# First maxima over 128 rows, and the layer-norm roots of later batches as Newton steps on VectorE

## What is computed

```python
def _layernorm(x, axis=-1, eps=1e-05):
    m = jnp.mean(x, axis=axis, keepdims=True)
    v = jnp.var(x, axis=axis, keepdims=True)
    return (x - m) / jnp.sqrt(v + eps)
...
        q = apply_rotary_emb(q, cos, sin)
        k = apply_rotary_emb(k, cos, sin)
...
        scores = jnp.einsum('bhid,bhjd->bhij', q, k, preferred_element_type=jnp.float32) * scale
        scores = jnp.where(causal, scores, -jnp.inf)
        probs = jax.nn.softmax(scores, axis=-1).astype(x.dtype)
        out = jnp.einsum('bhij,bhjd->bhid', probs, v, preferred_element_type=jnp.float32).astype(x.dtype)
...
    x = x + _layernorm(_L0_attn_ref(_layernorm(x, axis=-1), ...), axis=-1)
```

## Time and profile before

| | us |
|---|---|
| median of 3 runs | 1308.08 (1306.36 to 1308.83) |
| the profiled execution | 1310.2 |
| its span | 1308.5 |
| first scores of slot 0 | 87.35 |
| first scores of slots 1, 2, 3, 4 | 143.27, 203.29, 262.07, 320.32 |
| busy: PE, DVE, ACT, POOL | 1163.0, 996.1, 932.6, 950.4 |

### The profile page before, as it was taken

How to read it: one execution, slowest core, us unless ns; L and a number is a source line. 1 busy time by engine, 2 the same in 40 slices (tenths; PEclk the granted TensorE clock), 3 DMA queues, 4 the chain that set the end, 5 groups by cost and what they waited for, 6 DMA issues and landing times. The chain is left out here.

```text
span 1308.5 us, 34679 instructions
## 1 busy us (share of the span) xinstructions
PE 1163.0 (89%) x13520; PEld 784.9 (60%) x13520; DVE 996.1 (76%) x2157; ACT 932.6 (71%) x2057; POOL 950.4 (73%) x988
## 2 busy tenths in 40 slices
PE   4689999999999999999999999999997398898983
PEld 1236676666666676766666676766776254564651
DVE  7859787877878787877879787877843748786857
ACT  3168878778786878778787878779897565454543
POOL 3529988898888888898888889888675425554524
PEclk8559999999999999999999999999999599998997
DMA  6541515253351515253342515253200400000002
GB/s 197 125 119 44 131 37 128 67 130 85 80 130 34 130 35 130 66 130 76 89 118 46 131 35 130 66 130 81 52 3 3 135 2 1 2 1 0 0 1 65
DMA packets 50635, 96.91 MB, mean 74 GB/s; under 512 B 6704, under 2 KB 23344, under 8 KB 48432
## 3 DMA queue, kind: packets, MB, share of 16 engines
q1 hardware_dynamic: 50480, 94.81, 29.6%
HBM read 58.47 MB, written 34.60 MB: 71 GB/s over the span
## 5 line engine op out<-in xcount | busy, mean ns | idle before, releaser
L651 POOL TENSOR_TENSOR Plo<-P,Phi 128x512 f16<-128x512 f32 (+3 forms) x640 | 538.6, 868 | 141.3 <-ACT P L389 140.7
L386 ACT ACTIVATE Phi<-psS 128x512 f16<-128x512 f32 (+3 forms) x768 | 383.4, 499 | 162.5 <-PE psS L254 114.7
L389 ACT ACTIVATE P<-psS 128x512 f32<-128x512 f32 (+3 forms) x640 | 305.5, 478 | 0.0
L272 PE MATMUL psO<-V,Plo 128*128 128x65 f16 x2304 | 287.8, 194 | 0.0
L268 PE MATMUL psO<-V,Phi 128*128 128x65 f16 x2304 | 287.5, 192 | 0.0
L270 PE MATMUL psO<-V,Phi 128*128 128x64 f16 x2304 | 287.2, 192 | 0.0
L248 PE MATMUL psS<-Q,K 128*128 128x512 f16 (+3 forms) x768 | 251.4, 327 | 37.6 <-DVE Plo L509 32.0
L558 DVE TENSOR_REDUCE pmax<-psX 128x1 f32<-128x512 f32 x384 | 254.8, 684 | 25.8 <-PE psX L330 15.9
L251 PE MATMUL psS<-Q,K 65*128 65x512 f16 (+3 forms) x768 | 251.7, 328 | 0.0
L330 PE MATMUL psX<-K,Q 128*128 128x512 f16 (+5 forms) x768 | 232.1, 337 | 18.6 <-DVE pmax L558 7.0
L268 PEld LDWEIGHTS psO<-V,Phi 128*128 128x128 f16 x2304 | 218.7, 98 | 39.8 <-POOL Plo L651 4.1
(11 more groups left out here) (163 smaller groups left out, 2180.0 us busy)
## 6 DMA issues: line engine op xcount, KB each, us to landing
K<-k_way SPq DMA_DIRECT2D x48, 512.0 KB, 6.9
k_way<-HL SPq DMA_DIRECT2D x64, 256.0 KB, 3.9
q_way<-HL SPq DMA_DIRECT2D x60, 256.0 KB, 3.8
Q<-q_way SPq DMA_DIRECT2D x60, 256.0 KB, 7.1
Q<-q_way SPq DMA_DIRECT2D x15, 512.0 KB, 11.9
x<-in_x SPq DMA_DIRECT2D x4, 512.0 KB, 5.5
out<-x SPq DMA_DIRECT2D x8, 256.0 KB, 2.2
y<-in_x SPq DMA_DIRECT2D x3, 512.0 KB, 10.5
```

What stands on the lines that cost most here:

```text
L272: mm = nc.tensor.matmul(O, M.Plo[:, U % NP_, k * P:(k + 1) * P], V[:, HD:2 * HD + 1], start=False, stop=j == t, skip_group_check=True)
L386: nc.scalar.activation(M.Phi[:, U % NP_, 0:w], X, ACT.Exp, scale=SCALE)
L389: nc.scalar.activation(full, X, ACT.Exp, scale=SCALE).then_inc(S.exp_done, 1)
L651: nc.gpsimd.tensor_tensor(M.Plo[:, U % NP_, 0:w], M.P32[:, U % NP_, 0:w], M.Phi[:, U % NP_, 0:w], ALU.subtract).then_inc(S.lo_pool, 1)
```

## The change

- The maxima of heads 1, 2 and 3 before slot 0 contract all 128 rows; TensorE waits for the second copy of Q ahead of head 1. Head 0 keeps 64 rows.
- The bn_stats of the three later batches move from u = 4 to u = 45 of s = -1, behind the maxima.
- bn_aggr, root and shift of each of these batches become 16 small steps of DVE, one at the start of each step u = 4 to 19 of slots 0, 2 and 3. The inverse root is a guess made with integer arithmetic on the bits and four Newton steps of three instructions; each waits for the one before. ACT's Sqrt at s = -1 and DVE's reciprocal there are gone.
- `x_normal` moves from u = 26 to 33 of s = -1 (24 tiles) to u = 30 to 37 of slots 0, 2 and 3 (8 tiles each).
- The rotary sums of K of the second head group (two items) move from POOL to DVE.

```diff
-X_STATS, X_RECIPROCAL, X_NORMAL = 4, 9, 26
-
+X_STATS = 45
+X_ROOT = {1: (0, 4), 2: (2, 4), 3: (3, 4)}
+X_NORMAL = 30
+
+DVE_SUMS = 6
...
+def inverse_root(nc, M, then, tiles):
+
+
+    std, rstd, half = M.std[:, tiles], M.rstd[:, tiles], M.shift[:, tiles]
+    then(nc.vector.tensor_scalar(rstd.bitcast(I32), std.bitcast(I32), -0.5, ROOT_SEED, ALU.mult, ALU.add))
+    yield
+    for _ in range(NEWTON):
+        then(nc.vector.scalar_tensor_tensor(out=half, in0=rstd, scalar=-0.5, in1=rstd, op0=ALU.mult, op1=ALU.mult))
+        yield
+        then(nc.vector.tensor_tensor(half, half, std, ALU.mult))
+        yield
+        then(nc.vector.scalar_tensor_tensor(out=rstd, in0=half, scalar=1.5, in1=rstd, op0=ALU.add, op1=ALU.mult))
+        yield
...
                     h, k = a
+                    if (s, h, k) == (-1, 1, 0):
+                        pe.wait_ge(S.first_twin, 16)
...
-                    rows = HD if s < 0 else P
+                    rows = HD if s < 0 and h == 0 else P
...
             def x_normal(n):
+                act.wait_ge(S.x_root, n // TT)
...
-                if s == -1 and u == X_STATS:
-                    act.wait_ge(S.var_ready[0], 3)
-                    nc.scalar.activation(M.std[:, TT:NT], M.std[:, TT:NT], ACT.Sqrt).then_inc(S.std_ready[0], 1)
-                if s == -1 and X_NORMAL <= u < X_NORMAL + TT:
-                    if u == X_NORMAL:
-                        act.wait_ge(S.rstd_ready[0], 1)
-                    for k in range(B - 1):
-                        x_normal(TT + (B - 1) * (u - X_NORMAL) + k)
+                for batch in range(1, B):
+                    if s == X_ROOT[batch][0] and X_NORMAL <= u < X_NORMAL + TT:
+                        x_normal(batch * TT + u - X_NORMAL)
...
+            def x_root(batch):
+
+
+                tiles = slice(batch * TT, (batch + 1) * TT)
+                for t in range(batch * TT, (batch + 1) * TT):
+                    last = nc.vector.bn_aggr(M.mv[:, t, :], M.bn[:, t, :])
+                then(last)
+                yield
+                then(nc.vector.tensor_scalar(M.std[:, tiles], M.mv[:, tiles, 1], EPS, None, ALU.add))
+                yield
+                yield from inverse_root(nc, M, then, tiles)
+                nc.vector.scalar_tensor_tensor(out=M.shift[:, tiles], in0=M.mv[:, tiles, 0], scalar=-1.0,
+                                               in1=M.rstd[:, tiles], op0=ALU.mult, op1=ALU.mult).then_inc(S.x_root, 1)
...
-                        if s == -2:
+                        if r < DVE_SUMS:
                             taken(dve, item)
...
-                    variance(range(TT, NT))
-                    dve.wait_ge(S.consts, 3)
-                if s == -1 and u == X_RECIPROCAL:
-                    x_reciprocal()
+                    for t in range(TT, NT):
+                        last = nc.vector.bn_stats(M.bn[:, t, :], M.y[:, t, :])
+                    then(last)
+                for batch in range(1, B):
+                    if s == X_ROOT[batch][0] and u >= X_ROOT[batch][1]:
+                        next(roots[batch], None)
...
-                if s == -2:
+                if r < DVE_SUMS:
                     return
```

More of the change, by code:

```diff
@@ L29 @@
 BF16 = mybir.dt.bfloat16
+I32 = mybir.dt.int32
 ALU = mybir.AluOpType
@@ L45 @@
 EPS = 1e-5
+ROOT_SEED = float(0x5F3759DF)
+NEWTON = 4
 NEG = -1.0e30
@@ L575, in join_max @@
                     dve.wait_ge(S.aux_free[(number[last] - k) % NAUX], (number[last] - k) // NAUX + 1)
+                if s < 0:
+                    dve.wait_ge(S.consts, 3)
                 nc.vector.tensor_reduce(M.pmax[:, 1, :, 2:7:4], M.pmix[:, :, 0:2, 0:3], AX.X, ALU.max)
@@ L612, in out_scale @@
                                         ALU.mult).then_inc(S.out_scaled, 1)
+            roots = {batch: x_root(batch) for batch in range(1, B)}
             for half in range(2):
@@ L1476, in build @@
         S.norm_later = sem("norm_later")
+        S.x_root = sem("x_root")
         S.y_stats = sem("y_stats")
```

## The result

| | before | after |
|---|---|---|
| median, us (4 runs each) | 1307.83 (1306.36 to 1308.83) | 1320.49 (1319.35 to 1324.85) |
| the profiled execution | 1310.2 | 1319.53 |
| its span | 1308.5 | 1317.8 |

The ratio is 1.0103, interval 1.0088 to 1.0117: the changed kernel is slower by 12.7 us. Its lines have moved: first scores L248 → L269, maxima L330 → L353 with the mask at L334 → L357, the projections L304 → L325, exponentials L386 and L389 → L409 and L412, low parts L651 → L682, the later bn_stats L477 → L661, normals L438 → L462. The root is at L179 to L186, its shift at L529.

What follows compares the result with a forecast made beforehand. The prediction took TensorE to bound the kernel, at half clock in the start and with DVE, POOL and ACT close behind in the slots. Terms -7.0 + 16.8 + 4.8 = +14.6 on 1308.1 gave 1322.7 us, range 1309 to 1332.

Steps and rivals of the forecast that it cites:

- The start: Before slot 0: moved statistics and 128-row maxima together make slot 0 begin 7.0 us earlier, near 80.3; ends 4.2 and 8.7.
- Statistics: Before slot 0: without the 24 bn_stats, V's banks come free sooner and the second group of maxima starts 4.2 us earlier.
- 128 rows: Maxima of heads 1 to 3: full rows let TensorE's clock rise some 8 us into head 1, saving 2.8 us.
- products with the same columns cost the same at one clock: First maxima: going from 64 to 128 rows changes no product's cost at one clock; only the clock can change.
- The rival in which the clock stays low: Maxima before slot 0: no clock rise, the start gives only 4.2 us; +17.4 in all, 1325.5 us; chance 0.12.
- The roots: Steps 4 to 19 of slots 0, 2, 3: small DVE instructions wait for POOL's running one; together 16.8 us later.
- 0.64 x (18.14/16)/1.63: Slot 0's root steps: average rest of a running POOL instruction, 0.64 us, times POOL's running share at 1.63 us a step.
- The two equations for T: DVE-bound step time with a root: 1.63 us against 1.23 in slot 0, 1.80 against 1.40 in slots 2 and 3.
- the 1.2 us that I took off: Slots 2 and 3: DVE idles later in waiting for V, so the roots' 6.4 us become 5.2.
- The part without waits for POOL: Root steps at 0.20 us each, no lock: 2.1 us in slot 0, 1.2 in slots 2 and 3, 4.5 us together.
- The rival of missed gaps: Root steps: POOL's queue keeps DVE out, waits half as long again; roots 24.9 us, +22.7 in all, 1330.8; chance 0.11.
- The normals: Steps 30 to 37 of slots 0, 2, 3: ACT lacks room, 1.6 us each meets steps 40 to 48; 4.8 us later.

Runs made afterwards that it cites:

- a_rows64: The changed kernel with all first maxima contracted over 64 rows again, nothing else undone; 1325.12 us.
- a_rows65: The changed kernel with the first maxima of heads 1 to 3 over 65 rows instead of 128; 1322.80 us.
- a_reduce: The changed kernel with each of the 15 small root instructions replaced by a one-operand tensor_reduce of 8 elements, same waits; 1307.77 us.
- a_normals16: The changed kernel with the normals at steps 15 to 22 of slots 1, 3 and 4 instead of 30 to 37 of 0, 2 and 3; 1321.08 us.

## Why the prediction was right, and where its terms were off

The forecast was 1322.7 us and the median came out at 1320.49, +12.7 for +14.6.

**The start: -7.0 forecast, -8.34 measured.**
- *Statistics, -4.2.* a_rows64 has this part without the rows: 87.35 - 83.41 = 3.94. Right in size, not in every step. The wait for the second copy of Q cost nothing: head 1's first product starts at 52.00, right behind head 0's last (51.92). The queries landed 0.9 us later than before (first maximum at 41.95, not 41.07), so the second group came at 43.02, not 42.17: 3.39 us earlier. At the join it is 3.53 (84.02 less 80.49 in a_rows64). The last 0.41 us came where the prediction let all stay as before: the DMA of the maxima landed 1.8 us after its issue, and 2.2 us after it in the kernel before. The 24 bn_stats ended up where I put them, hidden:

```profile
76.23 4.73 DVE L661 BATCH_NORM_STATS2 bn_xy<-y 128x6 f32<-128x128 f32 x24
81.53 0.69 DVE L558 TENSOR_TENSOR R<-psX,cos 128x512 f32<-128x512 f32 x1 [0.57 <-DVE bn_xy L661]
```

  The first rotary item starts 2.52 us after the first scores, for 2.46 before: 0.06 us.
- *128 rows, -2.8, all of it the clock.* The sum was too small (4.40 measured) and its reason mostly wrong. The step that failed is the sentence that products with the same columns cost the same at one clock: a_rows65 shows 3.03 us from row heights alone, at 0.50. The timeline of the kernel before has it in head 0, where products of 128 columns start 0.22 us apart:

```profile
46.84 0.29 PE L334 MATMUL psX<-maskN,ident 128*128 128x128 bf16 x1
47.06 0.28 PE L330 MATMUL psX<-K,Q 64*128 64x128 f16 x1
47.28 0.29 PE L334 MATMUL psX<-maskN,ident 128*128 128x128 bf16 x1
```

  The clock did rise with 128 rows and not with 64 or 65, as forecast, at 54.5 us and not near 59 (63.4 less 4.2), but it was worth 1.37 us, about half of the 2.8: DVE then paced the maxima, as the sum had it, and the clock fell again twice, which it had not.
- *The rival in which the clock stays low* is out. It came from the Trainium skill (TensorE: Matmul & The Clock Gate, What's actually happening), which has the clock go by how busy TensorE has been recently. Here TensorE was busy for 2.50 of 2.50 us both in the changed kernel and in a_rows65, and only in the first did the clock then rise; a_rows65 stayed at 0.50 through 6.00 of 6.00 us too. Busy time alone doesn't decide here.

**The roots: +16.8 forecast, +18.2 measured.** Forecast 6.4, 5.2, 5.2, measured 6.89, 5.73, 5.58. The mechanism is shown by a_reduce and by the ends of the 45 instructions, each at the end of POOL's where POOL ran. The Trainium skill (SBUF — State Buffer, Who interferes with whom) has a vector instruction with two SBUF inputs contend with a GpSimd instruction that reads SBUF, and a tensor_reduce never. This trace and a_reduce agree: 0.57 us each against 0.149 to 0.163. The mean wait, 0.57 less the 0.16 undisturbed, is 0.41 us; the sum had 0.64 x (18.14/16)/1.63 = 0.45. That estimate, what is left of a running POOL instruction times the share in which one runs, was good within a tenth. It takes the steps to fall at random into POOL's instructions, which they don't: 8 of the 35 started within 0.12 us of the start of POOL's, so that the mean came out right with some luck. The two equations for T are also solved a little off; they give 1.65 and 1.79 us instead of 1.63 and 1.80, and the sum would have been 16.7. What made the total larger than forecast was the slot, not the wait: slots 2 and 3 absorbed less than the 1.2 us that I took off, and in slot 0 TensorE had so little to do that its clock fell. How much of the 6.89 us that is, no run separates; 0.76 of them stand in steps 20 to 24, behind the root's last step. The windows of 106 to 109 and of 109 to 112 us:

```profile
106.00:109.00 3.00, 1.27 (x14) 0.54 (x13) 2.93 (x6) 1.45 (x3) 3.00 (x3) 1.00 0.14 29
109.00:112.00 3.00, 2.83 (x16) 1.70 (x17) 3.00 (x6) 0.90 (x2) 2.61 (x3) 0.52 0.98 213
```

The part without waits for POOL, 4.5 us in the forecast, was 3.3. The rival of missed gaps (24.9) is out: L179 and L184 took 1080 ns at most, and no step of the root waited for more than one instruction of POOL. The 1748 ns of L579 are real, though: in the kernel before it started at 255.25 us and ended at 257.00, under three low parts of POOL in a row of which the last ended at 256.97.

**The normals: +4.8 forecast, 1.29 + 1.26 + 1.50 = 4.05 measured** (3 x 1.28 = 3.84 in steps 36 to 44). The place was right, ACT busy for all of steps 36 to 44, and the size a little high; where the missing 0.3 us of a slot was absorbed is open.

**The sum.** -8.34 + 18.2 + 4.05 = +13.9, less the 0.68 by which slot 2 of before was long by chance, is the +13.2 of the table. That it closes proves nothing, since its terms are differences of the table's own columns; what it has to answer to is the +12.7 of the medians. Errors of the three terms (-1.3, +1.4, -0.8) cancelled in part, which is luck: the total was more right than its parts.

## What to carry to other kernels

A chain of tiny VectorE instructions is priced by what GpSimd does beside it: with two SBUF operands count each as its own time plus what is left, on average, of a running GpSimd instruction, times the share of time in which one runs (here 0.41 us of waiting for 0.16 us of work), so join batches to have fewer, not smaller, of them. Moving a one-time job out of a stretch where an engine idles, into a loop in which every engine concerned has under a fifth of its time left, gave back more than it won here; look for the step in which all of the engines concerned have room, not only the one that does the job. In a run of matmuls keep one row height: padding K from 64 to 65 or 128 rows won 3.0 us here before the clock came into it.

## What the runs showed of the hardware that I had not expected

- Products of 64 and of 128 rows by turns: 0.22 us from start to start for 128 columns at 1.2 GHz; with 65 or 128 rows in place of 64, 0.10 to 0.11.
- TensorE's clock stayed at 0.50 for the 37.3 us of a_rows65, 6.00 of 6.00 us busy in a part of it; with 128 rows it rose 2.5 us after head 1's start in the changed kernel, after the same work. 65 rows took away the lost time between products and didn't raise the clock: these are two effects.
- The clock fell in the middle of slot 0 after TensorE was busy for only 1.27 of 3.00 us beside the root, and in slot 3 of a_normals16, where it was 0.75 over 13.7 us. Beside the root of slot 3 in the changed kernel, where TensorE was busy for 21.76 of 28.16 us, it stayed at 1.00.
- A tensor_scalar on 8 numbers is kept out by POOL too: 456 to 1080 ns on integers, and 936 ns once on f32, where two others took 161 and 163.
- A small instruction can wait for three of POOL's in a row: the copy L579, 1748 ns in the kernel before.
